# Routing two more sequences behind attention's last maximum, and normalising the second layer's input once per expert slot

## The chip, the cores and the metric

The program runs on one core of a Trainium2 chip. Its engines are TensorE (PE, matmuls; weight loads are listed as PEld), VectorE (DVE), ScalarE (ACT), GpSimd (POOL) and SyncE (SP, which issues DMAs). The metric is device time in microseconds (us) of one launch. The kernel before takes 681.1 us (median of three runs, 679.51 to 681.44).

## The reference

Two transformer layers in f32 on x of 4 sequences, 1024 tokens, 128 features (D).

```
x = x + attention(layernorm(x))      # 16 heads of 8, ALiBi bias, causal softmax, output projection Wo
x = x + experts(layernorm(x))        # 8 experts, see below
x = x + mixing(layernorm(x))         # softmax(tanh(q k / sqrt(D))) over the 4 sequences of one position
x = x + linear(layernorm(x))         # weight plus a pooled low-rank part
```

The experts stage gives each token to the expert with the highest logit. A token's place in its expert's queue is the running count over all earlier tokens of all sequences, and a place of 512 or more is dropped. A kept token takes `gate * W2(relu(W1(gate * layernorm(x)) + b1)) + b2` times the gate; a dropped one keeps x. Layer norm is `(x - mean) / sqrt(variance + 1e-5)`.

## The kernel before, in words

**Attention.** The 64 (sequence, head) pairs go through 16 groups n of four heads. For each group PE computes scores twice: once for row maxima (`max_scores`, L829, reduced by DVE, L933) and once for the exponentials (`scores`, L857, exponentiated by ACT, L973, masked on the diagonal by POOL, L1022). `weighted_sums` (L878) multiplies by the values. A group has 12 such units (`NU`). The order of PE's, ACT's, DVE's and POOL's work is a list, `ORDER`, that the function `plan` writes before the program is built. DVE works ahead: the maxima of the last group end before its exponentials do.

**Early work.** `EARLY_AT` and `FIRST_AT` put other work behind numbered units of attention (a tick counts units from group 5 on; group 15's last unit is tick 131). `EARLY_AT` repeats per sequence: reciprocals, division and the addition of the output bias for sequences 0 to 2. `FIRST_AT` carries sequence 0 through its whole routing, sends included, while attention runs.

**Routing.** A sequence is two chunks of 512 tokens (k = 0 to 7; `QC` = 2 chunks of `CH` = 4 tiles of 128 tokens). Its steps: `project` (PE, by Wo), `add` (DVE), `moments` (DVE: bn_stats and bn_aggr), `power` (POOL: the root of the variance by ALU.pow), `scales` (DVE: one Newton step, then minus mean times scale), `turned` (PE transposes), `columns` (ACT copies), `logits` (PE), `take`, `choose` (DVE: the expert), `exps` (ACT), `counts` (PE: running count), `place` (DVE: slot and gate), `gated` (ACT: gate times normalised row), and `send` (POOL: an indirect DMA of 128 rows to the slots in DRAM). Sequences 1 to 3 are routed after attention in a second program block. The order there is `ROUTE_ORDER`, from a planner with estimated times (`route_plan`). The two blocks are separated by a join of all engines (L459).

**Experts.** SP stores x to DRAM (L1422), loads it back in the order that mixing needs (L1428, 32 DMAs), waits for all 32 sends and loads the slots (L1431). For each of the 8 experts e, PE, ACT and DVE compute 512 rows `ye`; DVE's part is L1576 (add b2) and four of L1580 (times gate, plus x). SP stores each `ye` (L1435).

**Last stage.** POOL fetches each token's row by indirect DMA (L1469, 128 rows each, 32 of them; a dropped token keeps the x loaded before). Eight chunks j then pass through the steps of `last_plan`: `m0`, `p0`, `n0` (moments, root, scale of the first norm), `a0` (ACT applies it, L1898), `t3`, `x3`, `u`, `ut`, `s`, `te`, `mask`, `mixed`, `mix` (the mixing), `m1`, `p1`, `n1` (second norm), `t4`, `x4`, `f`, `add` (the linear part and the result). Each engine runs its own steps in the order of `LAST_ORDER` and waits where an input is missing.

Of the kernel before, what the change touches and what calls it, by code (L numbers as in the profile page):

```python
# [7 lines left out]
F32 = mybir.dt.float32  # L8
# [6 lines left out]
P = 128  # L15
# [4 lines left out]
CH = 4  # L20
# [18 lines left out]
XG, X1, GATE, ROW = 0, D, 2 * D, 2 * D + 1  # L39
# [92 lines left out]
EARLY_AT = {6: ["reciprocals"], 7: ["store_reciprocals"], 9: ["load_reciprocals"], 20: ["divide"], 21: ["divide"],  # L132
            23: ["bias"], 24: ["bias"]}
FIRST_AT = {28: ("project", 0), 34: ("project", 1), 40: ("moments", 0), 44: ("moments", 1), 50: ("power", 0), 56: ("scales", 0),
            57: ("centre", 0), 62: ("turned", 0), 64: ("logits", 0), 66: ("turned", 1), 68: ("logits", 1), 72: ("choose", 0), 73: ("exps", 0),
            75: ("counts", 0), 79: ("place", 0), **{84 + 2 * i: ("gated", i) for i in range(KB)}, **{87 + 2 * i: ("send", i) for i in range(KB)}}
RING_TIME = {"project": (1000, 600), "centre": (250, 200), "turned": (500, 600), "logits": (500, 200), "counts": (350, 230)}
# [23 lines left out]
def plan():  # L161
# [12 lines left out]
    while s_todo or a_todo or v_todo or t_todo:  # L174
# [65 lines left out]
        elif kind == "V":  # L240
# [14 lines left out]
            for name in EARLY_AT.get(tick, []) if 0 <= b < EARLY else []:  # L255
# [3 lines left out]
                pool += time * (engine == "pool")  # L259
            name, c = FIRST_AT.get((n - H // GH - 1) * NU + u, (None, 0))  # L260
# [32 lines left out]
def build(nc, x, Wq, bq, Wk, bk, Wv, bv, Wo, bo, Wr, br, W1, b1, W2, b2, W1q, W1k, Wf, disha, consts, out):  # L293
    ctx = ExitStack()
    with ctx:
# [19 lines left out]
        x1_dram = nc.dram_tensor("x1_rows", (B * S, D), F32).ap()  # L315
        y_dram = nc.dram_tensor("expert_out", (E * CAP, D), F32).ap()
# [17 lines left out]
        def part(shape, dt=F32):  # L334
# [9 lines left out]
            xn2=part([TILES, D]), xt2=part([2, CW]), st=part([2, CW]), rdb=part([S]),  # L344
            stats2=part([TILES, 6]), mv2=part([TILES, 2]), ve2=part([TILES]), rs2=part([TILES]), nt2=part([3, TILES]),
# [21 lines left out]
            sem(n) for n in ("lg_ready", "ex_ready", "hot_ready", "slot_ready", "row_ready", "scattered"))  # L367
        rden_out, rdb_in, e_chain, r_chain = sem("rden_out"), sem("rdb_in"), sem("e_chain"), sem("r_chain")
# [90 lines left out]
        with att:  # L459
# [342 lines left out]
            def _(pe):  # L802
# [79 lines left out]

                for kind, n, *args in ORDER:
                    if kind == "A":
                        max_scores(n, *args)
                    elif kind == "T":
# [34 lines left out]
            def _(dve):  # L921
# [21 lines left out]

                for kind, n, *args in ORDER:
                    if kind == "A":
                        maxima(n, *args)
                    elif kind == "E" and args[0] == "reciprocals":
# [15 lines left out]
            def _(act):  # L963
# [32 lines left out]
                for kind, n, *args in ORDER:  # L996
# [6 lines left out]
                    elif kind == "E" and args[0] in RING_TIME:  # L1003
# [5 lines left out]
                        nc.scalar.copy(dst, psS[:, bank, 0:dst.shape[-1]]).then_inc(ring_read, 1)  # L1009
                    elif kind == "E" and args[0] == "exps":  # L1010
                        act.wait_ge(lg_ready, 1)
                        nc.scalar.activation(r["ex"][:, 0:KB, :], r["lg"][:, 0:KB, :], ACT.Exp).then_inc(ex_ready, 1)
# [941 lines left out]
```

## Time and profile before

| | |
|---|---|
| three timed runs | 679.51, 681.1, 681.44 us |
| profiled execution, its own time | 678.24 us |
| its span, first to last instruction | 676.0 us |
| granted TensorE clock, mean | 0.913 |
| PE busy | 534.4 us (79%) |
| DVE busy | 501.2 us (74%) |
| ACT busy | 418.7 us (62%) |
| POOL busy | 234.8 us (35%) |

The profile shows one execution. The profiled execution's own time is 2.2 us above its span, since launch and end lie around it. Busy shares are averages over stages with different limits, so each stage is to be read by itself. The page's 40 slices are 16.9 us each; DVE's digits are

```profile
DVE  4999878889888888789895988889008732626796
```

and the two zeros are the end of attention, from 474.6 us on, where no maximum is left. The program's stages in this trace: attention to 503.8 us, routing to 560.9 us (end of the last send), experts to 587.4 us, the last stage from the first fetch at 590.3 us to the end at 676.0 us.

### The profile page before, as it was taken

The numbers are of one execution on the slowest core, as the hardware profiler recorded it, in microseconds if no ns is written. First come the engines' busy times: TensorE is split into PE (matmuls) and PEld (weight loads), VectorE is DVE, ScalarE is ACT, GpSimd is POOL, SyncE is SP. The second block draws the span as 40 slices with busy tenths as digits, with TensorE's granted clock in tenths as the row PEclk, the third lists the DMA queues.
The fourth block names the chain that finished last, engine by engine and source line by source line (L and its number), as shares of the span: only waits on it lengthen the run. The fifth ranks groups of instructions, "written<-read, shape, count | busy, mean of one in ns | idle before, by whom it ended". The sixth has DMA issues, their size and how long they took to land. (4 is left out here: it accounts for less than half of the span.)

```text
span 676.0 us, 13740 instructions
## 1 busy us (share of the span) xinstructions
PE 534.4 (79%) x4905; PEld 251.8 (37%) x4905; DVE 501.2 (74%) x1035; ACT 418.7 (62%) x737; POOL 234.8 (35%) x333
## 2 busy tenths in 40 slices
PE   3774798899999899998898888988867617957774
PEld 1441233333233223333333233333127615835563
DVE  4999878889888888789895988889008732626796
ACT  1971278787887787787786767867861412316651
POOL 2563012212212215222323224621621671078821
PEclk9886599999999999999999999989998757976897
DMA  7379355466533353121340120401013247310122
GB/s 181 88 175 280 99 128 119 116 149 196 145 83 68 67 114 67 39 42 31 68 89 19 41 56 28 121 20 37 10 25 114 71 136 284 111 28 21 35 48 63
DMA packets 66891, 61.11 MB, mean 90 GB/s; under 512 B 12121, under 2 KB 56058, under 8 KB 66812
## 3 DMA queue, kind: packets, MB, share of 16 engines
q1 hardware_dynamic: 58100, 53.93, 31.6%
q0 software_dynamic: 2560, 3.38, 1.7%
q10 hardware_dynamic: 6164, 2.94, 1.6%
q8 instruction: 39, 0.64, 0.4%
q14 instruction: 28, 0.23, 0.1%
HBM read 33.03 MB, written 29.85 MB: 93 GB/s over the span
## 5 line engine op out<-in xcount | busy, mean ns | idle before, releaser
L933 DVE TENSOR_REDUCE neg_max<-bank 128x2 f32<-128x1024 f32 (+2 forms) x320 | 341.4, 1113 | 62.8 <-PE bank L829 60.0
L973 ACT ACTIVATE probs<-ring 128x512 f32<-128x512 f32 (+4 forms) x480 | 301.8, 682 | 73.6 <-PE ring L857 62.7
L857 PE MATMUL ring<-q_operand,k_operand 56*128 56x512 bf16 (+3 forms) x768 | 161.7, 331 | 18.7 <-ACT probs L973 13.9
L878 PE MATMUL sums<-probs,v_all 128*9 128x512 f32 (+3 forms) x1536 | 161.5, 493 | 6.6 <-POOL probs L1022 4.3
L1022 POOL TENSOR_SCALAR_AFFINE_SELECT probs<-probs 128x512 f32<-128x512 f32 x128 | 80.5, 634 | 210.8 <-ACT probs L973 210.4
L829 PE MATMUL bank<-k_operand,q_operand 54*128 54x512 bf16 (+3 forms) x768 | 141.4, 340 | 9.1 <-DVE v_all L613 5.3
L857 PEld LDWEIGHTS ring<-q_operand,k_operand 56*128 56x128 bf16 x768 | 49.4, 94 | 146.0 <-ACT probs L973 103.9
L823 PE MATMUL bank<-masks 64*128 64x128 bf16 (+2 forms) x768 | 70.9, 225 | 6.8 <-DVE neg_max L933 5.8
L829 PEld LDWEIGHTS bank<-k_operand,q_operand 54*128 54x128 bf16 x768 | 46.0, 97 | 26.7 <-DVE neg_max L933 15.1
L823 PEld LDWEIGHTS bank<-masks 64*128 64x128 bf16 x768 | 36.2, 96 | 40.9 <-DVE neg_max L933 27.2
L1469 POOL DMA_INDIRECT early<-expert_out,back x32 | 32.7, 1022 | 38.3 <-issue 38.3
L878 PEld LDWEIGHTS sums<-probs,v_all 128*9 128x9 f32 x1536 | 23.5, 88 | 55.5 <-issue 42.8
L1514 DVE TENSOR_TENSOR rows<-rows,bank 128x512 f32<-128x512 f32 x6 | 4.1, 684 | 36.2 <-PE bank L1674 33.6
L980 ACT COPY max_rows_sb<-ring 32x128 bf16<-32x128 bf16 x32 | 8.0, 251 | 35.3 <-PE ring L840 35.0
L1898 ACT ACTIVATE xe<-early,nt 128x128 f32<-128x128 f32 x32 | 13.2, 482 | 24.6 <-issue 18.8
L1458 POOL DMA_INDIRECT expert_rows<-rows,early x24 | 23.6, 982 | 8.4 <-issue 6.6
L1036 POOL CAST max_parts<-low_max 128x16 bf16<-128x16 f32 x16 | 3.1, 196 | 66.4 <-DVE low_max L938 66.4
L1477 POOL TENSOR_TENSOR rs<-ve,half_pow 128x4 f32<-128x4 f32 x16 | 17.3, 1082 | 20.9 <-DVE ve L1595 20.7
L1589 DVE BATCH_NORM_STATS2 stats<-early 128x6 f32<-128x128 f32 x64 | 13.9, 279 | 14.0 <-DMA early<-expert_out,back 13.8
L986 ACT COPY osum<-sums 128x512 f32<-128x512 f32 x32 | 18.8, 588 | 7.7 <-PE sums L878 7.4
L840 PE MATMUL ring<-identb,max_parts 128*32 128x128 bf16 x32 | 7.1, 222 | 19.8 <-POOL max_parts L1039 19.1
L1856 ACT COPY early<-ring 128x512 f32<-128x512 f32 x6 | 3.5, 585 | 25.3 <-PE ring L1685 16.8
(208 smaller groups left out, 657.5 us busy)
## 6 DMA issues: line engine op xcount, KB each, us to landing
q_operand<-q_rows SPq DMA_DIRECT2D x64, 96.0 KB, 3.8
k_operand<-k_rows SPq DMA_DIRECT2D x32, 192.0 KB, 4.5
q_rows<-early SPq DMA_DIRECT2D x36, 128.0 KB, 2.4
k_rows<-early SPq DMA_DIRECT2D x36, 128.0 KB, 2.4
expert_rows<-fill SPq DMA_DIRECT2D x16, 257.0 KB, 4.2
rows<-expert_rows SPq DMA_DIRECT2D x8, 514.0 KB, 6.6
weighted_sums<-osum SPq DMA_DIRECT2D x126, 18.0 KB
sums_in<-in_L_attn_x SPq DMA_DIRECT2D x4, 512.0 KB, 7.3
```

The source lines that it names most:

```text
L823: nc.tensor.matmul(ends, masks[rows, 0, a, :], masks[rows, 1, a:a + 1, 64 * a:P].to_broadcast([64, len(pairs), P - 64 * a]), start=a == 0, ...
L829: last = nc.tensor.matmul(ps[:, h, w * j:w * j + w], q_op[rows, buf, t // CH, p, P * (t % CH):P * (t % CH) + P], k_op[rows, buf, p, CW * k ...
L857: last = nc.tensor.matmul(psS[:, bank, w * j:w * j + w], k_op[rows, buf, p, P * kb:P * kb + P], q_op[rows, buf, c, p, q0:q0 + w], start=Tr ...
L878: last = nc.tensor.matmul(psO[32 * i:32 * i + HD + 1, q0:q0 + w], v_all[:, n, kb, i, :], probs[:, u % NPROBS, i // 2, i % 2, 0:w], start=u ...
L933: nc.vector.tensor_reduce(neg_max[:, n % 2, slot, kc, :, pairs[0]:pairs[-1] + 1, t % CH], src, AX.X, ALU.max, negate=True).then_inc(a_read, 1)
L973: nc.scalar.activation(dst, src, ACT.Exp).then_inc(ring_read, 1)
L986: nc.scalar.copy(osum[:, slot, :], psO).then_inc(o_ready, 1)
L1022: nc.gpsimd.affine_select(out=tri, in_=tri, compare_op=ALU.is_ge, fill=0.0, base=0, pattern=[[0, GH], [1, P]], channel_multiplier=-1).then ...
L1458: nc.gpsimd.indirect_dma_start(out=slots_dram, out_offset=bass.IndirectOffsetOnAxis(ap=slot[:, u:u + 1], axis=0), in_=rows[:, u, :], in_of ...
L1469: nc.gpsimd.indirect_dma_start(out=x2[:, u, :], out_offset=None, in_=y_dram, in_offset=bass.IndirectOffsetOnAxis(ap=back[:, u:u + 1], axis=0),
L1477: nc.gpsimd.tensor_tensor(rs[:, z, c], ve[:, z, c], half_pow[:, 0:CH], ALU.pow).then_inc(root_ready[z], 1)
L1589: last = nc.vector.bn_stats(stats[:, z, u, :], x2[:, u, :])
```

## The change

Two things are changed.

1. **Sequences 1 and 2 are routed inside attention's block**, behind the last maximum. A table `TAIL_AT` puts `project` to `place` of chunks 2 to 5 at ticks 116 to 131. Their matmuls write to the PSUM banks of the maxima (`half[...]`), and DVE, not ACT, copies the columns. `gated` and `send` of these sequences stay in the second block, where they now stand first. The bias addition moves from ticks 23 and 24 to 11 and 12 of each sequence.
2. **The first norm of the second layer is computed per slot**, once, where `ye` is made. Rows get two more numbers, scale `RS` and minus mean times scale `MRS`, so slots are 259 floats wide, and rows of x and of `ye` in DRAM 130 floats (520 bytes) instead of 128. The steps `m0`, `p0` and `n0` leave the last stage, and `a0` takes its scale and shift from the fetched row. DVE computes moments and scales of the slots between the experts, with five roots on POOL, for the groups `NORMS`. A store of `ye` waits for its group's scales. The x rows in DRAM carry the routing norm's scales (a dropped token's row is unchanged, so is its norm), so SP's stores of x wait for the scales instead of for x. The load of x is 4 DMAs instead of 32.

```diff
-XG, X1, GATE, ROW = 0, D, 2 * D, 2 * D + 1
+XG, X1, RS, MRS, GATE, ROW = 0, D, 2 * D, 2 * D + 1, 2 * D + 2, 2 * D + 3
-EARLY_AT = {6: ["reciprocals"], 7: ["store_reciprocals"], 9: ["load_reciprocals"], 20: ["divide"], 21: ["divide"],
-            23: ["bias"], 24: ["bias"]}
+EARLY_AT = {6: ["reciprocals"], 7: ["store_reciprocals"], 9: ["load_reciprocals"], 11: ["bias"], 12: ["bias"], 20: ["divide"], 21: ["divide"]}
+TAIL_AT = {116: [("project", 2)], 117: [("project", 3), ("add", 2), ("add", 3), ("moments", 2)],
...
+           128: [("logits", 4)], 129: [("logits", 5), ("choose", 2)], 131: [("counts", 2), ("exps", 2), ("place", 2)]}
+                def late_project(k):
+                    if k == QC:
+                        pe.wait_ge(a_read, NG * NM)
...
+                    pe.wait_ge(at_ready, k + 1)
+                def late_turned(k):
+                    pe.wait_ge(x1_ready, k + 1)
...
+                def late_logits(k):
+                    pe.wait_ge(late_xt, k - QC + 1)
...
+                def late_counts(b):
+                    pe.wait_ge(hot_ready, b + 1)
...
-            sp.wait_ge(x1_ready, k + 1)
+            sp.wait_ge(scales_ready, 1 + [k in g for g in GROUPS].index(True))
...
-        for j in range(CHUNKS):
-            for q in range(B):
-                src = x1_dram[S * q:S * q + S, :].rearrange("(u t) d -> t u d", t=32)
-                sp.dma_start(x2[32 * q:32 * q + 32, CH * j:CH * j + CH, :], src[:, CH * j:CH * j + CH, :]).then_inc(x2_in[j], 16)
+        for q in range(B):
+            sp.dma_start(x2[32 * q:32 * q + 32, :, :], x1_dram[S * q:S * q + S, :].rearrange("(u t) d -> t u d", t=32)).then_inc(x2_in, 16)
...
-            sp.wait_ge(ye_ready, e + 1)
+            sp.wait_ge(ye_ready, 1 + [e in g for g in NORMS].index(True))
...
+    NORMS = [(0, 1), (2, 3), (4, 5), (6,), (7,)]
+        def slot_moments(e):
+            dve.wait_ge(ye_sum, e + 1)
+            for a in range(CH):
+                last = nc.vector.bn_stats(stats[:, 0, CH * e + a, :], ye[:, e, a, 0:D])
+            link(last)
+            for a in range(CH):
+                last = nc.vector.bn_aggr(mv[:, 0, CH * e + a, :], stats[:, 0, CH * e + a, :])
+            link(last)
+        for g, group in enumerate(NORMS):
+            for e in group:
+                expert_sum(e)
+                slot_moments(e)
+                if e == group[0] and g > 0:
+                    slot_scales(g - 1)
+            slot_variances(g)
+        slot_scales(len(NORMS) - 1)
...
         def apply_of(j):
-            act.wait_ge(nt_ready, j + 1)
+            act.wait_ge(y_in[j], 16 * CH)
```

Three places show what the planners and the new code make of it. In all of them `bank_0` and `bank_1` are the maxima's PSUM banks, `ring` the banks of the scores, `sums` those of the weighted sums.

PE at the end of attention, in the kernel before:

```order
L857 MATMUL ring<-q_operand,k_operand 128x384 x3
L878 MATMUL sums<-probs,v_all 9x128 x4
L857 MATMUL ring<-q_operand,k_operand 128x256 x4
L878 MATMUL sums<-probs,v_all 9x384 x4
L878 MATMUL sums<-probs,v_all 9x256 x4
L459 UNCONDITIONAL_BRANCH
```

The same place after the change (`wrc` is the router's weight, `incl` and `ones` the count's masks):

```order
L890 MATMUL sums<-probs,v_all 9x512 x4
L926 MATMUL bank_1<-wrc,early 128x8 x4
L869 MATMUL ring<-q_operand,k_operand 128x384 x3
L890 MATMUL sums<-probs,v_all 9x128 x4
L926 MATMUL bank_1<-wrc,early 128x8 x4
L869 MATMUL ring<-q_operand,k_operand 128x256 x4
L890 MATMUL sums<-probs,v_all 9x384 x4
L890 MATMUL sums<-probs,v_all 9x256 x4
L459 MATMUL bank_1<-early,incl 128x64
L461 MATMUL bank_1<-early,ones 128x64
```

Sequence 2's logits now stand between the last units, and its count behind the last weighted sum, ahead of the join.

POOL from the routing to the end, in the kernel before (`half_pow` marks a root, `expert_rows` a send, `expert_out` a fetch):

```order
L1458 DMA expert_rows<-rows,early 4096x257 x8
L1451 TENSOR_TENSOR early<-early,half_pow 128x4 x2
L1458 DMA expert_rows<-rows,early 4096x257 x16
L1469 DMA early<-expert_out,back 128x128 x8
L1477 TENSOR_TENSOR rs<-ve,half_pow 128x4
L1469 DMA early<-expert_out,back 128x128 x8
L1477 TENSOR_TENSOR rs<-ve,half_pow 128x4 x2
L1469 DMA early<-expert_out,back 128x128 x4
L1477 TENSOR_TENSOR rs<-ve,half_pow 128x4 x2
```

The same place after it:

```order
L1572 DMA expert_rows<-rows,early 4096x259 x9
L1565 TENSOR_TENSOR early<-early,half_pow 128x4
L1572 DMA expert_rows<-rows,early 4096x259
L1565 TENSOR_TENSOR early<-early,half_pow 128x4
L1572 DMA expert_rows<-rows,early 4096x259 x14
L1596 TENSOR_TENSOR rs<-ve,half_pow 128x8 x3
L1596 TENSOR_TENSOR rs<-ve,half_pow 128x4 x2
L1583 DMA early<-expert_out,back 128x130 x24
L1591 TENSOR_TENSOR rs<-ve,half_pow 128x4
L1583 DMA early<-expert_out,back 128x130 x8
L1591 TENSOR_TENSOR rs<-ve,half_pow 128x4 x7
```

The roots of the slots stand ahead of all fetches, one of the eight `p1` stands among the fetches, and seven stand behind them.

DVE among the experts, in the kernel before:

```order
L1576 TENSOR_TENSOR yb<-ring,b2b 128x512
L1580 SCALAR_TENSOR_TENSOR ye<-yb,rows 128x128 x4
L1576 TENSOR_TENSOR yb<-ring,b2b 128x512
L1580 SCALAR_TENSOR_TENSOR ye<-yb,rows 128x128 x4
L1576 TENSOR_TENSOR yb<-ring,b2b 128x512
```

The same place after it:

```order
L1691 TENSOR_TENSOR yb<-ring,b2b 128x512
L1695 SCALAR_TENSOR_TENSOR ye<-yb,rows 128x128 x4
L1702 BN_STATS stats<-ye 128x6 x4
L1705 BN_AGGR mv<-stats 128x2 x4
L1720 SCALAR_TENSOR_TENSOR nt<-ve,rs 128x8
L1721 TENSOR_TENSOR nt<-nt,rs 128x8
L1722 SCALAR_TENSOR_TENSOR ye<-nt,rs 128x8
L1723 SCALAR_TENSOR_TENSOR ye<-mv,ye 128x8
L1691 TENSOR_TENSOR yb<-ring,b2b 128x512
```

Between two experts' sums DVE now has four bn_stats and four bn_aggr each time, and in five places the four short operations that turn a root into scale and shift. These left the last stage, where they stood eight times as `m0` and `n0`.

## Rows read from the trace of the kernel before

**Rows 1.** Windows: busy time by engine, then granted clock, DMA share, GB/s.

```profile
400.00:474.60 74.60, 67.86 (x746) 25.35 (x746) 63.84 (x64) 57.21 (x99) 27.88 (x49) 0.98 0.20 51
476.00:503.80 27.80, 20.57 (x178) 4.72 (x173) 0.00 (x0) 22.09 (x38) 13.11 (x16) 1.00 0.08 18
571.07:587.43 16.36, 16.36 (x102) 13.08 (x101) 14.47 (x40) 7.05 (x11) 0.00 (x0) 1.00 0.49 188
590.32:640.50 50.18, 34.32 (x157) 25.16 (x155) 25.87 (x144) 22.52 (x47) 41.17 (x40) 0.76 0.12 28
640.50:676.00 35.50, 21.39 (x138) 17.55 (x138) 28.68 (x144) 13.13 (x26) 8.79 (x9) 0.88 0.23 53
```

**Rows 2.** Timeline, PE across the join: start, duration, operation, idle before.

```profile
502.49 0.62 PE L878 MATMUL sums<-probs,v_all 128*9 128x256 f32 x8 [0.37 <-POOL probs L1022]
505.24 0.76 PE L1705 MATMUL sums<-w1k,w1q 128*128 128x128 f32 x2 [2.13 <-PEq L459]
510.49 1.15 PE L1674 MATMUL bank<-wo,sums_in 128*128 128x128 f32 x8
511.48 0.60 PE L1685 MATMUL ring<-ident,rows 128*128 128x128 f32 x4
511.92 1.90 PE L1692 MATMUL ring<-wrc,early 128*128 128x8 f32 x16
```

**Rows 3.** Timeline, ACT's last stores of attention, then a `place` on DVE.

```profile
503.78 0.91 ACTq L991 DMA_DIRECT2D weighted_sums<-osum  x2
...
522.22 0.22 DVE L1308 TENSOR_REDUCE early<-early 128x8 f32<-128x64 f32 x1
...
524.05 0.16 DVE L1320 CAST early<-early 128x8 uint32<-128x8 f32 x1
```

**Rows 4.** Timeline, POOL in the routing: first send, root, next send, last send.

```profile
525.54 1.07 POOL L1458 DMA_INDIRECT expert_rows<-rows,early  x1 [1.50 <-ACT rows L1861]
...
535.61 1.05 POOL L1451 TENSOR_TENSOR early<-early,half_pow 128x4 f32<-128x4 f32 x1
...
540.70 1.04 POOL L1458 DMA_INDIRECT expert_rows<-rows,early  x1 [0.18 <-issue]
...
559.95 0.97 POOL L1458 DMA_INDIRECT expert_rows<-rows,early  x1 [0.30 <-issue]
```

**Rows 5.** Timeline, SP's queue: x loaded back.

```profile
542.15 19.14 SPq L1428 DMA_DIRECT2D early<-x_rows  x32
```

**Rows 6.** Timeline, DVE at the first expert and at the last two.

```profile
571.07 0.69 DVE L1576 TENSOR_TENSOR yb<-ring,b2b 128x512 f32<-128x512 f32 x1 [7.21 <-PE ring L1767]
...
583.80 0.68 DVE L1576 TENSOR_TENSOR yb<-ring,b2b 128x512 f32<-128x512 f32 x1
585.57 0.68 DVE L1576 TENSOR_TENSOR yb<-ring,b2b 128x512 f32<-128x512 f32 x1
```

**Rows 7.** Timeline, last stage: fetches on POOL, first norm's steps on DVE.

```profile
590.32 1.05 POOL L1469 DMA_INDIRECT early<-expert_out,back  x1 [29.40 <-issue]
...
595.59 1.00 POOL L1469 DMA_INDIRECT early<-expert_out,back  x1 [0.30 <-issue]
...
601.58 0.16 DVE L1601 SCALAR_TENSOR_TENSOR nt<-ve,rs 128x4 f32<-128x4 f32 x1 [3.32 <-POOL rs L1477]
...
602.25 0.86 DVE L1589 BATCH_NORM_STATS2 stats<-early 128x6 f32<-128x128 f32 x4
...
603.56 0.17 DVE L1595 TENSOR_SCALAR ve<-mv 128x4 f32<-128x4 f32 x1
```

**Rows 8.** Timeline, DVE late in the last stage: mask, norm steps, two results.

```profile
654.80 0.68 DVE L1609 TENSOR_TENSOR ee<-ee,samet 128x512 f32<-128x512 f32 x1
...
658.22 0.15 DVE L1601 SCALAR_TENSOR_TENSOR nt<-ve,rs 128x4 f32<-128x4 f32 x1
...
658.84 1.13 DVE L1631 SCALAR_TENSOR_TENSOR res<-ring,nt,early 128x128 f32<-128x128 f32 x4
...
671.35 1.12 DVE L1631 SCALAR_TENSOR_TENSOR res<-ring,nt,early 128x128 f32<-128x128 f32 x4 [0.74 <-PE ring L1833]
```

More of the change, by code:

```diff
@@ L259, in plan @@
                 pool += time * (engine == "pool")
+            for name, c in TAIL_AT.get((n - H // GH - 1) * NU + u, []):
+                assert not a_todo
+                order.append(("E", n, "late_" + name, c // QC, c))
+                pe += TAIL_PE[name] + 2 * DRAIN if name in TAIL_PE else 0
             name, c = FIRST_AT.get((n - H // GH - 1) * NU + u, (None, 0))
@@ L1228, in route_plan @@
         items["place", r] = ("dve", 2400, 0, [("counts", r), ("exps", r)])
-        items["gated", r] = ("act", 3800 if r < EARLY else 1900, 0, [("place", r)])
+        for i in range(QC if r < EARLY else 1):
+            items["gated", QC * r + i] = ("act", 1900, 0, [("place", r)])
         if r == EARLY:
@@ L1232, in route_plan @@
         for u in range(KB * r, KB * r + KB):
-            items["send", u] = ("pool", 1280, 0, [("gated", r)] if u < TILES - CH else [("gated_last", 0)])
-    for i in [(name, k) for name in ("project", "add", "moments", "turned", "columns", "logits", "take") for k in GROUPS[0]]:
+            items["send", u] = ("pool", 1280, 0, [("gated", u // CH)] if u < TILES - CH else [("gated_last", 0)])
+    for i in [(name, k) for name in ("project", "add", "moments", "turned", "columns", "logits", "take") for k in range(K0)]:
         del items[i]
-    for name in ("power", "scales", "choose", "exps", "counts", "place", "gated"):
-        del items[name, 0]
+    for i in [(name, b) for name in ("power", "scales", "choose", "exps", "counts", "place") for b in range(EARLY)] + [("gated", c) for c in range(QC)]:
+        del items[i]
     for u in range(KB):
@@ L1483, in _ @@
                 send_rows(i)
+        for g in range(len(NORMS)):
+            root_of_slots(g)
         for name, j in LAST_ORDER:
@@ L1573, in _, with expert_sum @@
         nc.vector.memset(xe[:, :, :, D:D + 1], 1.0)
-        for e in range(E):
+        def expert_sum(e):
             dve.wait_ge(y_psum, e + 1)
@@ L1587, in moments @@
+        for g, group in enumerate(NORMS):
[6 more added lines that the diff above has]
+        slot_scales(len(NORMS) - 1)
+        def moments(j):
             c = range(CH * j, CH * j + CH)
             for u in c:
-                last = nc.vector.bn_stats(stats[:, z, u, :], x2[:, u, :])
+                last = nc.vector.bn_stats(stats[:, 1, u, :], x2[:, u, 0:D])
@@ L1648, in _ @@
                 dve.wait_ge(x3_ready, j + 1)
-                moments(1, j)
+                moments(j)
             elif name == "add":
```

222 lines of the change are left out of this document (153 added, 69 removed).

## The prediction, made before the changed kernel was timed

> **What bounds the kernel now.** I read the page's slices first, then windows by stage, then the timeline of each engine at the borders of the stages. Four readings matter.
>
> In the end of attention DVE has nothing to do (0.00 us of 27.8), while PE is busy 20.57 us and ACT 22.09 us at a granted clock of 1.00 [rows 1]. In the body of attention PE is busy 67.86 of 74.60 us, a share of 0.91 [rows 1]. That is as full as PE gets in this code, so the end has some room, not much.
>
> The routing is bound by POOL. Its 24 sends begin at 525.54 us and end at 560.92 us; the last 16 start every (559.95 - 540.70) / 15 = 1.28 us [rows 4]. The first of them comes 20.3 us after PE's first instruction behind the join at 505.24 us [rows 2], because sequence 1 has first to be routed.
>
> The experts are bound by PE: it is busy all of 16.36 us at clock 1.00, DVE 14.47 us [rows 1]. DVE is close behind, and that is the important row: where it has work waiting, one expert costs it 585.57 - 583.80 = 1.77 us [rows 6].
>
> The last stage is bound by POOL first, 41.17 of 50.18 us, then by DVE, 28.68 of 35.50 us [rows 1]. Four fetches take 595.59 - 590.32 = 5.27 us [rows 7].
>
> **The change part by part.** Five terms.
>
> *1. The end of attention grows: +6.1 us.* PE gets four `project` of 511.48 - 510.49 = 0.99 us, four `turned` of 511.92 - 511.48 = 0.44 us, four `logits` of 1.90 / 2 = 0.95 us [rows 2], and two `counts`, nine small bf16 matmuls each, for which I have no row; a `logits` bounds one from above, 0 from below, and I take 0.4 us. That is 3.96 + 1.76 + 3.80 + 0.80 = 10.3 us. PE would have 20.57 + 10.3 = 30.9 us of work where it had 27.8 us of time. At the body's share of 0.91 this takes 33.9 us, so +6.1. If the work filled every gap it would be +3.1; if nothing of it were hidden, +10.3. DVE's adds, moments, copies and choices lie in its idle time. The inserted matmuls wait for DVE in between (transposes for `add`, `logits` for the copied columns). Queued behind such a wait on PE are scores, and ACT waits for those; one or two ticks between a step and the next hide most of that.
>
> *2. The join comes later: +1.0 us.* Before, PE's last weighted sum ends at 503.11 us, ACT's stores at 504.69 us (+1.6), and PE goes on at 505.24 us [rows 2, 3]. Now sequence 2's count (0.4) and then `place` on DVE (524.21 - 522.22 = 2.0) must follow the last weighted sum, since every engine meets at the join: +2.6 against +1.6. Bounds +0.5 and +3, the latter if `choose` of sequence 2 is late for its count.
>
> *3. The routing shrinks: -20.8 us.* From PE's first instruction behind the join to the end of the last send it took 560.92 - 505.24 = 55.7 us [rows 2, 4]. Now sequence 1 and 2 are placed when the block begins, and only ACT's `gated` stands ahead of the first send. A first send starts 525.54 - 524.05 = 1.5 us after the slot is written [rows 3, 4]; with 0.1 for the entry, 1.6 us. Then 24 sends at 1.28 (30.8) and two roots at 1.05 plus 0.2 (2.5) [rows 4]: 34.9 us. This holds only if sequence 3 keeps up. Following it from its denominators by durations like those above, its roots are due 11 and 13 us after the join, where POOL reaches them at 13 and 16 us, and its rows are gated at 24 us, where POOL wants them at 24.5. So there is almost no slack. Bounds -22 and -14.
>
> *4. The experts grow: +13.5 us.* DVE now needs per expert 1.77 [rows 6] plus four bn_stats and four bn_aggr, which took 603.56 - 602.25 = 1.31 us in `m0` [rows 7]: 8 x 3.08 = 24.6 us. Five additions of eps at 0.1 (0.5) and five groups of scales at 602.25 - 601.58 = 0.67 (3.35) [rows 7] follow. The last group's root is on POOL with nothing left to cover it: 1.05 [rows 4] plus 0.17 and 0.2 for hand-over. In all 29.9 us from DVE's first `yb` to the last `ye`, against 16.4 [rows 1, 6]. PE, at 2.2 us an expert, now waits for DVE. What is late next is every store of `ye`, and POOL's first fetch waits for all of them. Bounds +12.5 (all short operations overlapped) and +19 (PE slow as well).
>
> *5. The last stage shrinks: -11.7 us.* It took 676.0 - 590.32 = 85.7 us [rows 1, 7]. POOL's 32 fetches take 32 x 1.318 = 42.2 us and one root between them 1.25; the second `p1` ends at 44.6 us from the first fetch. In DVE's order `n1` of chunk 1 stands behind the mask of chunk 4, and everything behind it waits for that root. From there DVE has seven `n1` at 658.84 - 658.22 = 0.62 and seven `add` at 1.13, 12.3 us, and four times mask, `mix` and `m1`, 658.22 - 654.80 = 3.42 us each, less one mask of 0.7: 13.0 us [rows 8]. That is 69.9 us; 0.6 for the last root, and 3.5 us from the last result's end (672.47) to the end [rows 8], give 74.0 us. So the fetches are no longer the longer half: DVE's work piles up behind them, because POOL's order holds seven roots back. Bounds: -12.3 with no wait at all, -4 if PE sets the pace at a reduced clock.
>
> Edits at about nothing: the earlier bias additions (the same POOL work at other ticks; up to 1 us if a mask waits for it), five roots of the slots (the first four under DVE's next expert), rows of 259 instead of 257 floats, the x stores that wait for scales (chunks 0 to 5 have them at the block's start).
>
> The sum is 6.1 + 1.0 - 20.8 + 13.5 - 11.7 = -11.9 us. The profiled execution took 678.24 us, so 666.3 us by its own time. The median of the runs is 681.1 us, 2.9 above it; the same difference gives 669.2 us. I predict 669 us.
>
> **The rivals.**
>
> *A, slower than before: TensorE falls to its lower clock from the experts on.* PE was at 1.00 among the experts when always busy, and at 0.76 in the fetch half of the last stage when busy 34.32 of 50.18 us [rows 1]. Now DVE makes it wait at every expert, and the filler matmuls of the kernel stand only before and after. PE's work at full speed is 34.32 x 0.76 + 21.39 x 0.88 = 44.9 us in the last stage; at 1.2 GHz it takes 90 us, and the experts' 16.36 take 32.7. Then terms 4 and 5 are +16.3 and +4.1, and the time is 681.1 + 7.1 - 20.8 + 16.3 + 4.1 = 688 us. It turns slower than before once the last stage's mean clock is near 0.53; at 0.7 DVE still bounds it. Against it speaks that 0.76 was granted with PE no busier than it will be.
>
> The Trainium skill (TensorE: Matmul & The Clock Gate, "HAM oscillation — how this bites in real kernels") describes bursts of matmuls between waits that start at the lower clock each time. By that rule this rival's 688 us holds; the rows bear it out only in part.
>
> *B, the x rows come back late.* SP's 32 loads occupied its queue for 19.14 us [rows 5], partly issue, partly transfer. If the four large ones take as long, they start some 22 us after the join (last scales, then the store's landing) and end at 41, while the slots' loads want the DMA engines at 36. That delays the experts by 5 us: 674 us. For it speaks that the bytes are the same, against it that the DMA share was far from full.
>
> The Trainium skill (DMA: Bandwidth & Descriptors, "How a descriptor splits into AXI transactions") says that bytes before a start off a 256-byte boundary cost beats too; its 576-byte example takes 25 beats instead of 18. Rows of 520 bytes mostly start off such a boundary, rows of 512 never do, so it speaks for B and against the change. No row here shows it.
>
> *C, the end of attention hides nothing.* Term 1 is 10.3 and term 2 is 3.0, since PE is in order and waits for DVE and for POOL's roots behind masks: 675.5 us. ACT's room (22.09 of 27.8) speaks against, the many hand-overs for it.
>
> *D, B and C together:* 680.7 us, no change.
>
> **How the numbers follow.** Forecast 0.60, A 0.07, B 0.13, C 0.15, D 0.05. The forecast's own spread is about 662 to 676 us from the bounds of its terms. The range reaches down to 660 us (term 1 fully in the gaps, sends undisturbed) and up to 681 us, to C and D, and leaves out A. A difference under 0.3% (2 us) can't be told from none. Faster by more than that hold the forecast, B and C but for a little of each: 0.84. Same: D and that remainder, 0.07. Slower: A and the rest of D, 0.09.
>
> **What would show it.** In the profile after: PE busy some 31 us in a stretch of about 34 us at the end of attention; the last send's end near 547 us by the span; DVE busy nearly throughout the experts, some 30 us from first to last `yb`, with PE idle behind DVE; the first fetch at about 589 us, much where it was; seven roots behind the last fetch, DVE full from there, the end about 74 us after the first fetch. The prediction is wrong if DVE's work per slot overlaps PE's waits less or more than I say, if POOL waits between sends for sequence 3, or if the clock in the last stage is below 0.6.

## The result, and the profile after

| | before | after |
|---|---|---|
| median of 14 runs each | 679.44 us | 687.6 us |
| lowest to highest | 677.07 to 681.58 | 682.36 to 693.4 |
| profiled execution, its own time / span | 678.24 / 676.0 us | 693.4 / 691.5 us |

The ratio after to before is 1.011 (95%: 1.0084 to 1.0136): the change made the kernel 1.1% slower here, where I had forecast 669 us. The profiled execution is one of the three longest of the 14, which the ratio leaves out; a later trace of a typical execution (e0_fourth, below) shows the same. In later runs the same code took 669 to 670 us on two chips, 1% less than the kernel before there. That difference is what the experiments are about.

Four borders split the trace into the prediction's terms: PE's first instruction behind the join, the end of the last send, the first fetch, the end.

Timeline of after, PE and ACT at the join, then DVE's wait ahead of sequence 2's `place` (start, duration, operation, idle before):

```profile
509.07 1.47 PE L890 MATMUL sums<-probs,v_all 128*9 128x384 f32 x8 [0.22 <-POOL probs L1124]
510.82 1.04 PE L890 MATMUL sums<-probs,v_all 128*9 128x256 f32 x8 [0.28 <-POOL probs L1124]
...
512.53 0.91 ACTq L1089 DMA_DIRECT2D weighted_sums<-osum  x2
513.49 0.26 ACT L1111 ACTIVATE early<-early 128x64 f32<-128x64 f32 x1 [0.99 <-ACT osum L1084]
513.88 0.22 DVE L1425 TENSOR_REDUCE early<-early 128x8 f32<-128x64 f32 x1 [2.32 <-ACT early L1111]
...
516.20 0.77 PE L1845 MATMUL sums<-w1k,w1q 128*128 128x128 f32 x2 [3.92 <-PEq L471]
```

PE's last weighted sum ends at 511.86 us, 8.75 later than before, and PE goes on 10.96 us later [rows 2]. The last sum alone took 1.04 us for the 0.62 before, at a granted clock of 0.50 (1.2 GHz).

Timeline of after, POOL: last send, first fetch, the one root among the fetches, last fetch:

```profile
551.62 0.98 POOL L1572 DMA_INDIRECT expert_rows<-rows,early  x1 [0.30 <-issue]
598.09 1.10 POOL L1583 DMA_INDIRECT early<-expert_out,back  x1 [3.79 <-issue]
...
629.47 1.04 POOL L1591 TENSOR_TENSOR rs<-ve,half_pow 128x4 f32<-128x4 f32 x1 [0.37 <-DVE ve L1744]
...
639.87 0.99 POOL L1583 DMA_INDIRECT early<-expert_out,back  x1 [0.30 <-issue]
```

Windows of after (stretch, its length, then busy time of PE, PEld, DVE, ACT, POOL, the granted clock, DMA share, GB/s), the end of attention, the experts and both halves of the last stage, against [rows 1]:

```profile
476.00:511.90 35.90, 32.92 (x266) 14.41 (x267) 20.50 (x89) 21.62 (x37) 11.51 (x14) 0.91 0.06 14
564.50:595.10 30.60, 23.44 (x122) 18.03 (x120) 27.86 (x129) 7.05 (x11) 6.95 (x5) 0.94 0.21 80
598.09:640.90 42.81, 13.74 (x56) 10.33 (x56) 3.90 (x17) 9.41 (x20) 33.07 (x33) 0.66 0.13 26
640.90:691.50 50.60, 34.98 (x228) 28.50 (x228) 35.27 (x168) 25.31 (x52) 8.71 (x7) 0.87 0.18 43
```

The third row is the surprise. POOL's fetches run as forecast, but beside them PE is busy 13.74 us and DVE 3.90, where [rows 1] had 34.32 and 25.87. From 640.90 us on the three engines do the work that should have lain beside the fetches. Where they stood still is in the timelines of PE, ACT and DVE in that stretch:

```profile
617.37 0.71 PE L1953 MATMUL bank<-xe,ee 128*128 128x129 f32 x4
617.88 1.06 PE L1953 MATMUL ring<-xe,ee 128*128 128x129 f32 x4
618.74 1.91 PE L1943 MATMUL bank<-ut,xt 128*128 128x128 f32 x8
620.45 0.95 PE L1929 MATMUL bank<-ident,xe 128*128 128x128 f32 x4
```

```profile
618.39 1.65 ACT L2037 ACTIVATE xe<-early 128x128 f32<-128x128 f32 x4
639.19 0.60 ACT L2058 ACTIVATE th<-bank 128x512 f32<-128x512 f32 x1 [19.15 <-remote]
...
643.45 0.58 ACT L2048 COPY xt<-bank 128x512 f32<-128x512 f32 x1 [3.00 <-remote]
```

```profile
614.46 0.69 DVE L1756 TENSOR_TENSOR ee<-ee,samet 128x512 f32<-128x512 f32 x1 [19.35 <-ACT ee L2063]
626.45 0.17 DVE L1763 RECIPROCAL inv<-bank 128x2 f32<-128x2 f32 x1 [11.31 <-issue]
```

ACT's `th` of chunk 1 (L2058) needs the scores that PE's L1943 has finished, by the records, at 620.65 us. It starts at 639.19. DVE's first mix (L1763) needs the sums of L1953, finished at 618.94, and starts 7.5 us later. ACT's next copy needs the transposes of L1929 (621.40) and starts at 643.45, 22 us behind them and 2.6 us behind the end of the last fetch (640.86). So what depends on PE's products comes late, in PE's order, and the profile names no releaser ("remote" and "issue" are what it writes where it finds none). These late starts are called stops below.

### The profile page after: what moved, and what is told of

Its sections match the earlier page's. It is cut to its first block and busy times, and to the rows that moved or that the text cites. A ratio compares the mean times of both kernels' runs of the same rounds, so it can differ in the third digit from the quotient of the medians.

```text
span 691.5 us, 13695 instructions
## 1 busy us (share of the span) xinstructions
PE 534.7 (77%) x4905; PEld 249.0 (36%) x4905; DVE 503.2 (73%) x1020; ACT 415.6 (60%) x733; POOL 233.7 (34%) x330
## 5 line engine op out<-in xcount | busy, mean ns | idle before, releaser
L869 PE MATMUL ring<-q_operand,k_operand 56*128 56x512 bf16 (+3 forms) x768 | 161.8, 333 | 15.7 <-ACT probs L1071 11.9
L890 PE MATMUL sums<-probs,v_all 128*9 128x512 f32 (+3 forms) x1536 | 163.4, 498 | 4.8 <-POOL probs L1124 3.0
L2037 ACT ACTIVATE xe<-early 128x128 f32<-128x128 f32 x32 | 13.2, 487 | 26.4 <-DMA early<-expert_out,back 26.4
L1756 DVE TENSOR_TENSOR ee<-ee,samet 128x512 f32<-128x512 f32 x8 | 5.5, 687 | 31.3 <-ACT ee L2063 20.2
L1936 PE MATMUL bank<-xt,aqk 128*128 128x512 f32 x16 | 9.6, 684 | 19.1 <-ACT xt L2048 16.0
L1881 PE MATMUL bank<-sel,ident 128*128 128x256 f32 x48 | 13.8, 456 | 11.3 <-DMA early<-expert_out,back 11.3
L1591 POOL TENSOR_TENSOR rs<-ve,half_pow 128x4 f32<-128x4 f32 x8 | 9.8, 1219 | 35.8 <-DVE ve L1744 35.8
```

Source lines behind the costliest of these rows:

```text
L869: last = nc.tensor.matmul(psS[:, bank, w * j:w * j + w], k_op[rows, buf, p, P * kb:P * kb + P], q_op[rows, buf, c, p, q0:q0 + w], start=Tr ...
L890: last = nc.tensor.matmul(psO[32 * i:32 * i + HD + 1, q0:q0 + w], v_all[:, n, kb, i, :], probs[:, u % NPROBS, i // 2, i % 2, 0:w], start=u ...
L1881: nc.tensor.matmul(bank[:, CW // 2:], ident[:, :], sel[:, 0:2, :].rearrange("p c m -> p (c m)"), start=True, stop=True)
L2037: last = nc.scalar.activation(xe[:, j % XE, i, 0:D], x2[:, u, 0:D], ACT.Identity, bias=x2[:, u, D + 1:D + 2], scale=x2[:, u, D:D + 1])
```

## The experiments

All runs below come with runs of the kernel before on the same chip. The chips are numbered; that of the first 14 runs is not known. Stage times are read from each profile at the four borders, and "last" is from the first fetch to the end, in us. The recorded expectations number the theories of the stops: 1, an unbroken run of indirect fetches makes them; 2, a real dependence, such as rows that have not landed; 3, they come with the routing part; 4, they belong to a chip or to what happens on it at the time; 5, they come and go on any chip; 6, competing transfers make them. A quiet chip is one on which the changed kernel shows none.

| run | chip | median us | before there | ratio (95%) | last stage |
|---|---|---|---|---|---|
| e0_again (the changed kernel) | 13 | 670.35 | 675.61 | 0.991 (0.987 to 0.995) | 73.4 |
| e0_second (same) | 6 | 669.01 | 676.52 | 0.991 (0.987 to 0.994) | 73.6 |
| e0_third (same) | 6 | 669.6 | 676.42 | 0.990 (0.987 to 0.993) | 73.5 |
| e0_fourth (same) | 1 | 688.97 | 679.04 | 1.014 (1.007 to 1.021) | 88.2 |
| e1_gaps | 13 | 676.76 | 675.61 | 1.001 (0.998 to 1.004) | 81.3 |
| e1_second (same) | 6 | 675.96 | 676.42 | 1.000 (0.997 to 1.003) | 80.6 |
| e1_third (same) | 1 | 681.23 | 679.04 | 1.003 (1.000 to 1.005) | 81.6 |
| e2_routing_only | 13 | 666.94 | 675.61 | 0.988 (0.984 to 0.992) | 86.3 |
| e2_second (same) | 6 | 667.01 | 676.52 | 0.988 (0.985 to 0.992) | 85.8 |
| e3_norm_only | 13 | 677.91 | 675.61 | 1.004 (1.001 to 1.006) | 73.3 |
| e6_exps_first | 6 | 665.79 | 676.52 | 0.987 (0.983 to 0.991) | 85.6 |
| e6_second (same) | 6 | 667.13 | 676.42 | 0.987 (0.984 to 0.991) | 85.0 |
| e6_third (same) | 1 | 668.99 | 679.04 | 0.986 (0.981 to 0.991) | 86.2 |
| e7_flood | 6 | 674.33 | 676.42 | 0.998 (0.996 to 1.000) | 77.6 |
| e8_held | 1 | 691.12 | 679.04 | 1.020 (1.014 to 1.026) | 92.6 |
| e8_second (same) | 2 | 687.33 | 677.46 | 1.013 (1.009 to 1.018) | 91.8 |

**The changed kernel again: e0_again, e0_second, e0_third, e0_fourth.** No edit.

> The changed kernel once more, with nothing altered. Its profiled run had 93.4 us from the first fetch to the end, where ScalarE stood still 19.15 us in front of the second chunk's first exponential (620.04 to 639.19) and VectorE 7.5 us in front of the first mix, though TensorE's products had ended at 620.65 and 618.94. If these stops come from chance (a disturbed execution), this run has a last stage of 74 to 80 us and no stop over 3 us. If they belong to the kernel, ScalarE stops again in the stretch in which GpSimd issues 24 fetches without a break, and the time is 682 to 694 us, with a wider spread than that of the kernel before.

> The changed kernel a third time, unaltered. Its first runs took 687.6 us (682.4 to 693.4), its second ones, on another chip, 670.4 us (668.5 to 672.4), with no stop of ScalarE or VectorE and a last stage of 73.4 us. Theory 1 (the stops belong to the kernel's 24 fetches in a row) has lost by that, unless the chip matters too. Theory 4 (some chips deliver TensorE's signals late while GpSimd issues indirect transfers, others do not): either about 670 us with no stop, or 682 to 693 us with stops behind TensorE in the fetch stretch, and on a chip of the second kind the kernel before too has small stops in its runs of sends. Theory 5 (the state comes and goes on any chip): this run and the kernel before disagree about the stops though they share the chip.

> The changed kernel, unaltered, on whatever chip comes. On two chips it took 670.4 and 669.0 us without a stop (before: 675.6 and 676.5), on the chip of its first runs 687.6 us with stops of 19.2 and 7.5 us. Theory 4 (it depends on the chip or its load): near 669 us without stops, or 682 and more with them.

> The changed kernel, unaltered. Four profiled executions of it are known: one with stops behind TensorE's products (693.4 us), three on two other chips without (672.4, 667 to 671 us). Theory 4 (late signals belong to the chip or to what ran there then): near 669 us without stops on a quiet chip, 682 and more with them on another.

Chips 13 and 6 show no stop, chip 1 shows them again. ACT's waits behind PE in the fetch stretch of e0_second (total us, times, longest):

```profile
ACT xt L2048 <- PE bank L1929: 4.7, 2, 4.5
ACT ut L2053 <- PE bank L1936: 2.4, 2, 1.2
ACT th L2058 <- PE bank L1943: 1.2, 2, 0.8
```

and the timelines of ACT and DVE in e0_fourth:

```profile
634.91 0.60 ACT L2058 ACTIVATE th<-bank 128x512 f32<-128x512 f32 x1 [12.78 <-remote]
...
637.72 0.59 ACT L2048 COPY xt<-bank 128x512 f32<-128x512 f32 x1 [1.56 <-remote]
639.17 0.59 ACT L2068 COPY xt<-ring 128x512 f32<-128x512 f32 x1 [0.86 <-remote]
```

```profile
627.11 0.17 DVE L1763 RECIPROCAL inv<-bank 128x2 f32<-128x2 f32 x1 [10.22 <-remote]
```

The same instructions wait as in the first trace. So the stops are no single disturbed execution, and the code alone does not make them: theory 4 stands. Theory 5 has nothing for it, since chip 6 was quiet on both occasions and chip 1 showed stops in more than one kernel; but chip 1 was seen on one occasion only, so whether they belong to the chip or to that time is not shown. In both traces the root among the fetches (629.47 us in the first, 630.12 in e0_fourth) lies inside ACT's long wait and did not end it: ACT went on 8.7 and 3.8 us behind the root's end.

**The kernel before on a quiet chip: b_before.** No edit; one timed run, 675.34 us, on chip 6.

> The kernel before, unaltered, for its trace on the same chip as the changed one. In the trace known so far ScalarE stopped 8.5 us in the routing (528.66 to 537.15) and VectorE 2.5 us, with waits put down to nothing visible. Theory 4: on a chip where the changed kernel has no stops, this one has none either, the 8.5 us become about 3, and the time is 673 to 677 us; on a chip where the changed kernel stops, they are there, at 677 to 682 us.

It met the expectation. In the trace on which the prediction rests ACT had waited 8.49 us ahead of chunk 7's columns; here it is 3.58. First the known trace, then this one:

```profile
537.15 0.58 ACT L1856 COPY early<-ring 128x512 f32<-128x512 f32 x1 [8.49 <-remote]
```

```profile
530.83 0.58 ACT L1856 COPY early<-ring 128x512 f32<-128x512 f32 x1 [3.58 <-PE ring L1685]
```

So the trace of before already had a stop of this kind, in its run of 8 sends in a row; there ACT and DVE went on 0.5 us behind the end of the next root. Its stages on chip 6: join 503.8, routing 52.8, experts 30.7, last 85.8 us. The kernel before was not traced on chip 1.

**Gaps between the fetches: e1_gaps, e1_second, e1_third.**

```
                 fetch(j)
+                if j < CHUNKS - 1:
+                    nc.gpsimd.tensor_tensor(spare[:, j, :], half_pow[:, 0:CH], half_pow[:, 0:CH], ALU.pow)
```

> The changed kernel, with one 128x4 power on GpSimd behind each of the first seven fetch groups (four rows of slots each), written to a tile that nobody reads: 7 x about 0.95 us more on GpSimd. Theory 1 (an unbroken run of indirect fetches on GpSimd holds back TensorE's signals, or whatever ScalarE and VectorE need in order to go on): the powers break the run as the roots of the kernel before did, the stops shrink to 1 to 3 us, the last stage takes 76 to 84 us instead of 93.4, and the time is 672 to 680 us. Theory 2 (ScalarE waits for rows that have not landed, or for another real dependence): the powers only make the last fetch later by 6.7 us, the time is 687 to 695 us.

> The powers between the fetch groups once more. Without stops in the changed kernel on this chip it costs 6.5 us, as on the first occasion (676.8 against 670.4). With stops, theory 1 (the unbroken run of fetches turns late signals into long stops) expects it to win 5 to 12 us over the changed kernel; theory 4 alone (late signals whatever GpSimd does) expects it to lose by the same 6.5 us or gain nothing.

> Powers between the fetch groups. On a chip where the changed kernel has no stops: 6.5 us above it, 676 us. On a chip where it has them: theory 1 (the unbroken run of fetches makes the stops long) expects 5 to 12 us below the changed kernel, theory 4 alone at or above it.

Each power took 1.05 us, not the 0.95 expected. On quiet chips the seven cost 6.4 us. On chip 1 they win 7.7 us (681.2 against 689.0), and the last stage is 81.6 us, as on the quiet ones. ACT's `th` there waits 0.39 us. Windows of the fetch half and the rest, first e0_fourth, then e1_third, both on chip 1:

```profile
598.20:641.70 43.50, 18.69 (x66) 13.15 (x67) 4.17 (x17) 12.53 (x27) 33.52 (x33) 0.66 0.13 26
641.70:686.40 44.70, 31.43 (x221) 25.39 (x219) 34.81 (x167) 22.21 (x46) 8.58 (x7) 0.96 0.21 49
```

```profile
598.03:648.60 50.57, 30.83 (x164) 23.52 (x165) 16.19 (x72) 25.82 (x55) 41.77 (x40) 0.84 0.13 28
648.60:679.60 31.00, 18.25 (x123) 14.73 (x121) 23.28 (x112) 8.94 (x17) 7.78 (x7) 0.88 0.27 62
```

With one power behind every four fetches DVE does 16.19 us of work in the fetch half, without them 4.17. The ten runs with powers (679.0 to 683.2 us) lie below all four without (684.8 to 690.9). So theory 2 fails, which expects powers only to cost, and theory 1 stands in a narrower form: on chip 1 powers of 1.05 us between groups of four fetches took the long stops away. What in the powers does it is not isolated: they break the run of fetches, but they also slow the fetches down and move them against PE's work, and the single root of the changed kernel did not end a stop.

**One part of the change at a time: e2_routing_only, e2_second, e3_norm_only.** The first keeps the new routing inside attention's block and restores the per-token mean and deviation with its roots between the fetches; the second restores the old routing and keeps the per-slot norm. The lines are shortened to what changes; e2 keeps the wider rows of x and their four loads.

```
 e2:  -("landed", ...), ("a0", ..., ["landed"], ...)
      +("landed", ...), ("m0", "dve", ...), ("p0", "pool", ...), ("n0", "dve", ...), ("a0", ..., ["n0"], ...)
      -slot_moments(e); slot_variances(g); slot_scales(g - 1); root_of_slots(g)
 e3:  -TAIL_AT = {116: [("project", 2)], ...}      +TAIL_AT = {}
      -K0 = K1 = QC * EARLY                        +K0, K1 = QC * EARLY, QC
```

> Only the first part of the change: sequences 1 and 2 are routed behind attention's last maximum, the rows carry deviation and shift up to the router, but the mean and deviation of the second layer's first normalization are computed per token in the last stage, as before. By the traces the routing part moves the join by +11.0 us and shortens the routing by 19.3 us, and the last stage keeps its roots between the fetches: theory 1 expects 679.4 + 11.0 - 19.3 = 671 us (668 to 675), and a last stage of 84 to 88 us from the first fetch. Theory 3 (the stops of ScalarE come with the routing part, say by where the instructions now lie) expects stops of 5 us and more in the last stage here too, and 680 us or more.

> The routing part alone again (the first time 666.9 us, ratio to before 0.988). It keeps roots between the fetches. On a chip without stops: 665 to 669 us. On a chip with stops, theory 1 in its narrower form (an unbroken run of fetches is what turns a late signal into a long stop) expects at most 5 us more, 668 to 674 us, where the changed kernel has 682 or more; if the roots between the fetches don't matter it loses 10 us or more as well.

> Only the second part of the change: mean and deviation per slot behind each expert, carried in the rows; the routing as before. From the last send to the first fetch the traces show 29.4 us before and 45.5 us after (+16.1), and the last stage 85.7 and 93.4 us (+7.7). Theory 1: both come with this part, 679.4 + 23.8 = 703 us (697 to 707), with a stop of ScalarE of 10 us or more while 24 fetches run. Theory 3 (the stops come with the routing part): the last stage takes 74 us, 679.4 + 16.1 - 11.7 = 684 us.

The routing part alone is worth 8.7 and 9.5 us on chips 13 and 6. I had expected 671 us from terms of the first traces; it took 667, since the baseline was 4 us lower there. The norm part alone costs 2.3 us (677.9 against 675.6), not the 24 that theory 1 expected of a chip with stops: on chip 13 there were none, its experts took 43.8 us and its last stage 73.3. So the two parts nearly add up: 8.7 less 2.3 is 6.4 us, and e0_again gained 5.3 on the same chip. By the terms of the prediction the norm part was to cost 13.5 - 11.7 = 1.8 us and cost 2.3; the routing part was to win 20.8 - 7.1 = 13.7 us and won 8.7 and 9.5. Neither run fell on chip 1.

**Sequence 2's exponential ahead of the last copy: e6_exps_first, e6_second, e6_third.** On top of the routing part alone.

```
-           131: [("counts", 2), ("exps", 2), ("place", 2)]}
+           131: [("counts", 2), ("place", 2)]}
                     elif kind == "O":
+                        if n == NG - 1 and args[0] == QC - 1:
+                            (wait for lg_ready, then ex = Exp(lg) of sequence 2)
                         sums_out(n, *args)
```

> The routing part alone, and sequence 2's exponential on ScalarE put ahead of the copy and the two stores of attention's last sums instead of behind them. In the trace of the routing part alone VectorE waited 2.32 us for it (508.80 to 511.12) and its placement ended at 512.96, 2.3 us behind the last store's issue (510.69), and all engines wait for it at the join. If the join waits for that placement, it moves from 513.4 to about 511.5 and the time falls by 1.5 to 2 us, to 665 us. If the routing behind the join is set by something else (SyncE's load of the last denominators and what hangs on it), the time is the same within 0.5 us.

> The routing part alone with sequence 2's exponential ahead of attention's last copy, again: 665.8 us and a ratio of 0.987 to before the first time. If that holds, 664 to 667 us on a chip without stops, and it is the fastest of all versions; on a chip with stops 670 us or more, still ahead of the changed kernel by 10 us.

> The routing part alone with the exponential ahead of the last copy: 665.8 and 667.1 us before, 1.3 % below the kernel before on both occasions. Quiet chip: 665 to 668 us. Chip with stops: the roots between the fetches leave TensorE's signals gaps, 670 to 675 us, below the changed kernel by 10 us or more.

PE's wait at the join falls by 1.5 us. Timeline of PE behind the join, e2_routing_only, then e6_exps_first:

```profile
513.45 0.77 PE L1849 MATMUL sums<-w1k,w1q 128*128 128x128 f32 x2 [3.92 <-PEq L471]
```

```profile
514.04 0.77 PE L1853 MATMUL sums<-w1k,w1q 128*128 128x128 f32 x2 [2.42 <-PEq L471]
```

The median on chip 6 falls from 667.0 to 665.8 us on the one occasion on which both ran; the repeat gave 667.1, so the gain in time is not settled. On chip 1 its last stage is as quiet as elsewhere (86.2 us): with roots between the fetches this version is 20 us below the changed kernel there, 669.0 against 689.0. That speaks against theory 3, for it has the routing part. Its routing on chip 1 does take 36.3 us from the join to the last send's end, against 33.9 on chip 6, and POOL waits 2.37 us for sequence 3 as in the first trace. It is the best of all on chip 1, where e2 did not run, and not told apart from e2 elsewhere.

**Transfers beside the first fetches: e7_flood.**

```
+        act.wait_ge(y_out, 16 * E)
+        for i in range(2):
+            act.dma_start(flood_dram[i], x1_dram[:, :]).then_inc(flooded, 16)
```

> The changed kernel, and ScalarE issues two copies of x_rows (2.1 MB each, DRAM to DRAM) when the last slots' rows are stored, so that the DMA engines are busy during the fetches. Theory 6 (the stops come from transfers that compete with the fetches or with the loading of instructions): stops of ScalarE and VectorE appear behind TensorE's products though these are done, 5 us or more, put down to nothing visible. Its rival (transfers only delay transfers): the fetched rows land later and ScalarE's waits on them grow, by 2 to 10 us in the last stage, but every hop from TensorE to ScalarE stays under 0.5 us.

ACT's wait for the first fetched rows grew from 26.4 to 35.9 us, the last stage from 73.5 to 77.6, and ACT's longest wait behind PE's scores stayed at 3.6 us, with none put down to nothing:

```profile
ACT xe L2039 <- DMA early<-expert_out,back: 35.9, 1, 35.9
...
ACT th L2063 <- PE bank L1945: 7.0, 4, 3.6
```

Windows of e7_flood from the first fetch on (the number before the last is the DMA share):

```profile
594.20:604.00 9.80, 0.00 (x0) 0.00 (x0) 0.00 (x0) 0.00 (x0) 7.67 (x8) 0.50 1.01 325
604.00:614.00 10.00, 3.73 (x11) 3.09 (x12) 0.00 (x0) 1.65 (x4) 7.56 (x9) 0.54 0.51 161
614.00:624.00 10.00, 6.92 (x40) 4.66 (x38) 1.98 (x7) 6.52 (x15) 7.87 (x8) 1.00 0.14 30
```

The busy DMA engines delayed the first rows, by 9.5 us. But the copies had ended by the time PE made its first product of a chunk (L1931 at 614.38 us), so no hop from PE to ACT or DVE was tried while the engines were full. Theory 6 is left open by this run, and it was not tried on chip 1. What speaks against it is the DMA share while ACT stood still: 0.14 in the first trace, 0.12 in e0_fourth.

**The stops put in by hand: e8_held, e8_second.** 32 idle copies on ACT ahead of `th` of chunk 1, 16 on DVE ahead of the first mix (ACT's part is shown).

```
+                if j == 1:
+                    for i in range(32):
+                        act.wait_ge(held_act, i)
+                        nc.scalar.copy(hold[:, 0, :, :], rows[:, 0:CH, X1:X1 + D]).then_inc(held_act, 1)
```

> The changed kernel with the two stops of its first trace put in by hand: 32 idle copies of 128x512 (about 0.6 us each, 19 us) on ScalarE in front of the second chunk's exponentials, and 16 on VectorE (5 to 11 us) in front of the first mix. If those two stops are what made the last stage 93.4 us instead of 73.4, this kernel has a last stage of 91 to 95 us and 687 to 691 us on a quiet chip. If the rest of the excess came from elsewhere (the stop was partly hidden behind the fetches, which go on without ScalarE), the last stage is 80 to 88 us.

> The two stops put in by hand once more. The first time the chip was one on which the changed kernel stops by itself, and the idle copies lay over its own stops: last stage 92.6 us, 691.1 us, against 88.2 and 689.0 us without them. On a quiet chip there are only the stops put in: if ScalarE's 19 us and VectorE's are what the last stage of the first trace lost, it takes 88 to 94 us here instead of 73.5, and the kernel 683 to 690 us; if much of such a stop is hidden behind the fetches, it takes 80 to 86 us.

The first fell on chip 1, where the copies lay over the kernel's own stops, and says little. The second ran on chip 2. The changed kernel itself did not run there, but this trace shows no stop besides those put in:

```profile
615.56 20.76 ACT L2063 COPY hold<-rows 128x512 f32<-128x512 f32 x32
```

```profile
594.08:636.00 41.92, 13.70 (x56) 9.72 (x56) 10.36 (x32) 27.43 (x50) 32.57 (x33) 0.66 0.13 26
636.00:685.90 49.90, 35.41 (x228) 28.98 (x228) 35.74 (x168) 26.64 (x55) 9.13 (x8) 0.88 0.19 44
```

The last stage takes 91.8 us. PE's 13.70 us in the fetch half and 35.41 behind it are those of the first trace (13.74 and 34.98). Against the 73.5 us of the quiet chips the copies cost 18.3 us, for 20.8 us on ACT (and 7.35 on DVE). The first trace lost 19.9. So stops of that length at those two places are enough for all but 1.6 us of the excess, and hardly any of ACT's is hidden. What each of the two costs alone is not separated, nor does this run say why the real ones come.

## Why the prediction was wrong, step by step

Each term with its measurement, in the first traces and on chip 6 (b_before and e0_second), in us:

| term | forecast | first traces | chip 6 |
|---|---|---|---|
| 1 and 2, join | +7.1 | 505.24 to 516.20: +11.0 | +10.0 |
| 3, routing | -20.8 | 55.7 to 36.4: -19.3 | 52.8 to 34.2: -18.6 |
| 4, experts | +13.5 | 29.4 to 45.5: +16.1 | 30.7 to 44.9: +14.2 |
| 5, last stage | -11.7 | 85.7 to 93.4: +7.7 | 85.8 to 73.6: -12.2 |
| sum | -11.9 | +15.5 | -6.6 |

*Term 5 is the step that failed*: forecast -11.7 us, measured +7.7 in the first traces. "From there DVE has seven `n1`" and the work of four chunks, I wrote, and took for granted that chunks 0 to 3 are mixed beside the fetches. In the first trace DVE had mixed one when the last fetch was issued. The missing 19.4 us (93.4 against 74.0) are ACT's and DVE's stops behind finished products of PE. So the price of taking up PE's products was put at nothing while 24 fetches ran. On quiet chips the term is right to 0.6 us: four chunks are mixed before the last fetch, seven roots stand behind it, and DVE is busy 23.23 of the 30.9 us left in e0_second, for the 25.3 that I had counted. It is not full there.

What had spoken of this in the profile of before was ACT's wait of 8.49 us put down to "remote" (its row stands beside b_before), in a run of eight sends without a root. The prediction does not ask why its input, ready 5.5 us earlier, was not taken. The change took the roots out of the fetch loop, and 4 to 8 fetches in a row became 24. None of the rivals had this mechanism; A's 688 us is near the result by chance, since its clock of 0.53 did not come: the experts ran at 0.94, the last stage was at 0.66 and 0.87, and those with stops show the lower clock while PE had nothing to do.

*On quiet chips 669 us was met by luck.* The kernel before took 675.6 and 676.5 us there, not the 681.1 from which I counted, and the change won 5.3 to 7.5 us of the 11.9 forecast. Chip 6's row of -6.6 says where the other 5.3 went: 2.9 at the join, 2.2 in the routing and 0.7 in the experts, less 0.5 that the last stage gave.

*Terms 1 and 2* were 3 to 4 us short. Term 1: the last weighted sum ended 8.75 us later in the first trace and 7.75 on chip 6 (509.39 against 501.64), for 6.1 forecast. In the first trace PE's share of busy time was 32.92 / 35.90 = 0.92, about as taken, but its work was 32.9 us for the 30.9 forecast, at a granted clock of 0.91 where [rows 1] had 1.00. On chip 6 the clock stayed at 1.00, so the clock can account for the microsecond between the two, not for the rest; PE was busy 29.78 of 33.40 us there, a share of 0.89. Term 2: PE goes on 2.2 us later behind that sum, in both, for 1.0 forecast. That is `exps` of sequence 2, which stands behind ACT's two stores: `place` waited 2.32 us for it, and e6 took 1.5 us of it back. I had counted `place` but not what its other input is queued behind.

*Term 3* held: the send end is 34.2 us behind the join on chip 6 (34.9 forecast), and 36.4 where PE's products are late and POOL's root waited 2.51 us for sequence 3. The forecast gain of 20.8 was taken against 55.7 us, 2.9 of which were stops that chip 6 doesn't have.

*Term 4* held within 1 us on chip 6: from DVE's first `yb` to the last `ye` it took 30.9 us for the 29.9 forecast, DVE was busy 28.1 of them and PE waited for it. In the first trace PE's first transposes also came 5.3 us behind the issue of the slots' loads, 4.3 before; +16.1 is inside the bounds.

*Rival B* (x rows late) did not come: the four large loads took 4.8 us of SP's queue and the slots' loads started 1.5 us behind the last send. *Rival C* came in part, with 11.0 of its 13.3 us.

What stays open: what in chip 1, or beside the kernel on it, delays PE's products while POOL issues indirect transfers; why powers behind every four fetches prevent the stops while the one root in the changed kernel did not end them; and whether PE itself is late there (its recorded ends are modelled) or only its signals are. Both fit the order in which the waits end.

## What to carry to other kernels

A wait of an early trace that nothing visible releases is a risk, not noise: ask what was running without a break then, and whether the change makes that run longer. Short other work on GpSimd between groups of indirect transfers cost 6.4 us where nothing was wrong and won 7.7 where it was; the version that kept its own roots there had no long stop either. Take the changed kernel to a second chip before its mechanism is explained from one trace. And when a forecast time is met, compare the difference too: here 669 us was met with half of the gain.

## What was not expected of the hardware

- The same code took 669.0 to 670.4 us on chips 6 and 13, and 689.0 us on chip 1 (one occasion), while the kernel before differed by 0.5% between them (675.6, 676.5, 679.0 us).
- On chip 1, and in the first traces, ACT and DVE took up products of PE up to 22 us after their recorded end, in the stretches in which GpSimd issued indirect transfers; the latest came 2.6 us behind the last of them. The signals from ACT and DVE to PE in that stretch came within 0.1 us (in e0_fourth DVE's mix ended at 628.50 us and PE's transposes of it began at 628.56).
- At the end of attention the granted clock of the same code fell in some executions and not in others. In the first trace it was 1.00 up to 500 us and 0.67 in the next 5 us, with PE busy 3.71 of the 5 us before; in e0_second PE was busy 3.61 of the same 5 us and the clock stayed at 1.00.
